# Attention head order and GpSimd's split: values of block 0 ahead of its scores, and a split that waits for the softmax

## The reference

```
hs = scan over 32 steps: GRU(h, x[:, t])                    # h0 = cond
q, k, v = hs @ Wq + bq, hs @ Wk + bk, hs @ Wv + bv          # 4 heads of 64
x = x + softmax(q k^T / 2) v @ Wo + bo                      # over the 32 steps
qs = scan over 32 steps: RK4(q, p, x[:, t], tanh(q) @ C^T)  # q0 = p0 = cond
x = x + bitlinear(silu(bitlinear(qs, Wg)) * bitlinear(qs, Wu), Wd)
```

## Time and profile before

| what | us |
|---|---|
| median of 3 runs | 613.3 |
| lowest and highest run | 613.23, 615.46 |
| profiled execution, its time | 614.01 |
| profiled execution, its span | 612.1 |
| TensorE busy | 578.9 (95%) |
| VectorE busy | 517.3 (85%) |
| ScalarE busy | 404.3 (66%) |
| GpSimd busy | 255.3 (42%) |

### The profile page before, as it was taken

How to read it: one execution, slowest core, us unless ns; L and a number is a source line. 1 busy time by engine, 2 the same in 40 slices (tenths; PEclk the granted TensorE clock), 3 DMA queues, 4 the chain that set the end, 5 groups by cost and what they waited for, 6 DMA issues and landing times.

```text
span 612.1 us, 14221 instructions
## 1 busy us (share of the span) xinstructions
PE 578.9 (95%) x4924; PEld 525.0 (86%) x4924; DVE 517.3 (85%) x1545; ACT 404.3 (66%) x982; POOL 255.3 (42%) x401
## 2 busy tenths in 40 slices
PE   9999999999999889988888999999999999999997
PEld 8999999999999878877776888887887887888885
DVE  3777677676777768898988999999999999999996
ACT  3554444545444456577446888988888888888785
POOL 0423233332322453420144455565565565565550
PEclk9999999999999999999999999999999999999999
DMA  8400000000000000500000000000000000000001
GB/s 264 175 3 1 1 2 2 1 1 2 1 1 1 19 1 1 187 1 1 2 0 2 10 11 18 19 16 12 19 19 11 19 18 9 18 20 11 18 19 35
DMA packets 12518, 14.88 MB, mean 24 GB/s; under 512 B 1632, under 2 KB 10144, under 8 KB 12448
## 3 DMA queue, kind: packets, MB, share of 16 engines
q1 hardware_dynamic: 12448, 13.97, 6.7%
HBM read 9.78 MB, written 4.19 MB: 23 GB/s over the span
## 4 chain that ended last, share of the span: by engine, by line
PE 71%; ACT 13%; DVE 12%; issue 3%; DMA 1%; POOL 0%; SPq 0%; DVEq 0%; ACTq 0%
PE PS L452 23%; PE PS L314 17%; PE PS L337 12%; ACT q_s L763 4%; PE PS L504 4%; PE PS L525 3%; ACT k_s L744 2%; PE PS L488 2%; PE PS L373 2%; ACT big L676 2%; PE PS L430 2%; PE PS L390 2%; DVE PS L1062 1%; DVE big L944 1%; ACT PS L747 1%
## 5 line engine op out<-in xcount | busy, mean ns | idle before, releaser
L452 PE MATMUL PS<-k_s,h_s 128*128 128x128 f32 x1024 | 160.8, 285 | 4.4 <-DVE PS L1042 1.9
L452 PEld LDWEIGHTS PS<-k_s,h_s 128*128 128x128 f32 x1024 | 131.7, 191 | 21.8 <-DVE PS L1050 9.8
L314 PE MATMUL PS<-part 128*128 128x256 f32 x900 | 115.6, 286 | 0.0
L314 PEld LDWEIGHTS PS<-part 128*128 128x128 f32 x900 | 109.8, 191 | 0.0
L744 ACT ACTIVATE k_s<-h_s 128x128 f32<-128x128 f32 x256 | 69.1, 306 | 50.6 <-DVE h_s L1147 29.1
L337 PE MATMUL PS<-big,wrk 128*128 128x128 f32 x744 | 88.4, 275 | 1.7 <-DVE big L901 1.7
L337 PEld LDWEIGHTS PS<-big,wrk 128*128 128x128 f32 x744 | 85.8, 192 | 2.3 <-DVE big L901 2.3
L1215 POOL COPY h_s<-big 128x256 f32<-128x256 f32 x32 | 21.4, 669 | 129.5 <-DVE big L901 129.5
L452 PE MATMUL PS<-h_s 128*128 128x128 f32 x384 | 74.2, 275 | 0.0
L452 PEld LDWEIGHTS PS<-h_s 128*128 128x128 f32 x384 | 58.3, 192 | 0.0
L641 ACT ACTIVATE big<-big 128x256 f32<-128x256 f32 x32 | 13.3, 416 | 63.2 <-DVE big L883 63.2
(11 more groups left out here) (188 smaller groups left out, 1273.1 us busy)
## 6 DMA issues: line engine op xcount, KB each, us to landing
out<-q_s SPq DMA_DIRECT2D x32, 128.0 KB, 1.7
x_s<-in_xT SPq DMA_DIRECT2D x14, 256.0 KB, 6.0
k_s<-in_wgT SPq DMA_DIRECT2D x1, 832.0 KB, 5.5
k_s<-in_wuT SPq DMA_DIRECT2D x1, 832.0 KB, 7.1
k_s<-in_wih SPq DMA_DIRECT2D x3, 256.0 KB, 4.5
wrk<-in_whh SPq DMA_DIRECT2D x3, 256.0 KB, 4.8
h_s<-in_wdT SPq DMA_DIRECT2D x1, 768.0 KB, 6.8
x_s<-in_xT SPq DMA_DIRECT2D x4, 128.0 KB, 4.0
```

The costliest lines, as they stand in the source:

```text
L314: r = pe.matmul(p, y, x, start=i == 0, stop=i == len(passes) - 1)
L452: return pe.matmul(PS[:, m, 0:128], w, x, start=False, stop=True, skip_group_check=True)
```

## The change

On TensorE, `values(0, 0)` is issued ahead of `scores(0)`. Its passes are reordered in all blocks, so that the four with the high part of the states come first and the two with the low part last; only in block 0 is there a wait for the low part between them. ScalarE copies the values of block 0 ahead of its scores. ScalarE now drains three of the four `last` banks (`last[0]`, `last[2]`, `last[3]`) and VectorE one (`last[1]`), after the low part of block 0's states. GpSimd's split `i`, for `i` from 1, additionally waits for `s_P >= i`, that is for the scaling of block `i - 1`, and its constants for `s_P >= 8`.

```diff
--- before.py
+++ after.py
@@ -365,8 +365,8 @@
                 if i:
                     pe.wait_ge(s_sc, i)
                 else:
-                    pe.wait_ge(s_qk, 62)
-                    pe.wait_ge(s_qka, 2)
+                    pe.wait_ge(s_qk, 61)
+                    pe.wait_ge(s_qka, 3)
                 for g in range(4):
                     for hd in range(4):
                         a, kk, at, u = 64 * (hd % 2), hd // 2, (4 * i + g) * 128, unit(g, hd)
@@ -378,15 +378,19 @@
                 hi, lo = v_hi[i % 2], v_lo[i % 2]
                 if (i, hf) == (0, 0):
                     pe.wait_ge(s_wv, 2)
-                    pe.wait_ge(s_vs0, 2)
+                    pe.wait_ge(s_vs0, 1)
+                    pe.wait_ge(s_qka, 1)
                 elif hf == 0:
                     pe.wait_ge(s_split, i)
                 if (i, hf) != (0, 0):
                     pe.wait_ge(s_V, 2 * i + hf)
                 for g in (2 * hf, 2 * hf + 1):
-                    passes = [(x[:, k, g * 128:(g + 1) * 128], w[:, k, :]) for k in range(2)
-                              for x, w in ((lo, wv_hi), (hi, wv_lo), (hi, wv_hi))]
+                    at = slice(g * 128, (g + 1) * 128)
+                    passes = [(hi[:, k, at], w[:, k, :]) for w in (wv_lo, wv_hi) for k in range(2)]
+                    passes += [(lo[:, k, at], wv_hi[:, k, :]) for k in range(2)]
                     for n, (x, w) in enumerate(passes):
+                        if (i, g, n) == (0, 0, 4):
+                            pe.wait_ge(s_vs0, 2)
                         r = pe.matmul(PS[:, 4, (g % 2) * 256:(g % 2) * 256 + 256], raw(x), raw(w), start=n == 0,
                                       stop=n == 5)
                 r.then_inc(s_Vp, 1)
@@ -431,8 +435,11 @@
                 r.then_inc(s_o, 1)
 
             for i in range(10):
+                if i == 0:
+                    values(0, 0)
                 if i < 8:
                     scores(i)
+                if 1 <= i < 8:
                     values(i, 0)
                 if i == 8:
                     feats_of(7)
@@ -654,12 +661,13 @@
             ac.activation(wsum[:, 3:4], ones[:, 0:1], ACT.Exp)
             ac.wait_ge(s_hb, T)
             ac.activation(raw(v_hi[0]), h_s[:, :, 0:512], ACT.Copy).then_inc(s_vs0, 1)
-            for u in last[2:]:
+            for u in (last[0], last[2], last[3]):
                 kind, j, i = u
-                dst = k_s[:, i % 2, :].rearrange("p (b t) -> p t b", t=T)[:, 2 * j:2 * j + 2, :]
+                w, m = divmod(i, 2)
+                dst = (q_s, k_s)[w][:, m, :].rearrange("p (b t) -> p t b", t=T)[:, 2 * j:2 * j + 2, :]
                 ac.wait_ge(s_bulk, number[u] + 1)
                 ac.activation(dst, bulk_bank(u).rearrange("p (t b) -> p t b", t=2), ACT.Identity,
-                              bias=ba[:, 1, i % 2:i % 2 + 1]).then_inc(s_qka, 1)
+                              bias=ba[:, w, m:m + 1]).then_inc(s_qka, 1)
 
             def keep_values(i, hf):
                 if i >= 2 and hf == 0:
@@ -704,8 +712,11 @@
                 if i == 8:
                     keep_feats(7)
                 if i < 8:
+                    if i == 0:
+                        keep_values(0, 0)
                     keep_scores(i)
-                    keep_values(i, 0)
+                    if i:
+                        keep_values(i, 0)
                     if i in (5, 6):
                         weight_round(i - 5)
                     if i:
@@ -913,10 +924,9 @@
                         ve.wait_ge(ld_x[(n + 2) // 2], 32)
                     at = (n + 2) * 256 + col
                     ve.tensor_copy(raw(x_hi[n % 2][:, :, col:col + B]), x_s[:, :, at:at + B]).then_inc(s_xhi, 1)
-            for u in last[:2]:
-                qk_out(u)
             ve.wait_ge(s_vs0, 1)
             ve.tensor_tensor(raw(v_lo[0]), h_s[:, :, 0:512], v_hi[0], ALU.subtract).then_inc(s_vs0, 1)
+            qk_out(last[1])
 
             def maximum(i):
                 ve.wait_ge(s_sc, i + 1)
@@ -1227,11 +1237,13 @@
             po_.wait_ge(s_hb, T)
             for r in range(2):
                 po_.memset(PT[r][:, :, :], 0.0).then_inc(s_zero, 1)
+
             for i in range(9):
                 if i < 7:
                     src, hi, lo = h_s[:, :, (i + 1) * 512:(i + 2) * 512], v_hi[(i + 1) % 2], v_lo[(i + 1) % 2]
                     if i:
                         po_.wait_ge(s_Vp, 2 * i)
+                        po_.wait_ge(s_P, i)
                     po_.tensor_copy(raw(hi), src).then_inc(s_vhi, 1)
                     if i == 0:
                         po_.wait_ge(s_bulk, number[last[-1]] + 1)
@@ -1240,6 +1252,7 @@
                 if i == 8:
                     po_.wait_ge(ld_coup, 16)
                     po_.wait_ge(s_Vp, 16)
+                    po_.wait_ge(s_P, 8)
                     po_.tensor_scalar(coupU, coup, U, 0.0, ALU.mult, ALU.add).then_inc(s_cp, 1)
                     for dst, f in ((id_q1, (1 - kap) / c4), (id_s2, -kap / c4), (id_z3, (2 - 2 * kap) / c4)):
                         po_.tensor_scalar(dst, ident[:, :], f, 0.0, ALU.mult, ALU.add).then_inc(s_cp, 1)
```

## The result

The changed kernel takes 611.94 us (median of 8 runs, 611.07 to 612.34), the kernel before 613.75 (8 runs, 613.23 to 615.48). The ratio is 0.9961 with a 95% interval of 0.9947 to 0.9975. That is 1.5 to 3.3 us faster, around 2.4. The ratio weighs every run and lies near that of the means (614.15 and 611.78); the medians alone differ by 1.8. The span of the profiled execution went from 612.1 to 609.5.

The account below looks back on a forecast made before the run. TensorE was taken to bound the middle of the attention stage, the only stage that can change. Terms +0.37 - 1.68 + 0 = -1.31 us, from a median of 613.3, gave 612.0 us; range 610.9 to 613.9.

Parts of the forecast that it names:

- The head: Start of the attention stage: scores 0 0.55 us later, 0.18 regained; +0.37 us in sum, carried through blocks 2 to 4.
- the 0.18 for the scaling: Block 0's softmax scaling on VectorE: 0.69 us instead of 0.87 once GpSimd's split waits, gaining 0.18.
- Block 4: Softmax scaling freed of GpSimd's subtraction, so L430 in block 5 comes earlier: 1.68 us gained.
- the 0.53 behind it: L430 in block 5 was to follow L410 by 0.53 us, as in the pair a block later.
- The end: Block 7: scaling loses 0.44 us of blocking, but VectorE then waits for ScalarE's copy; gain 0, bound 0 to 0.4.
- the wait of 0.1: A 0.1 us wait was to reappear at the L430 after block 5's, hidden by the chain through ScalarE and VectorE.
- The price of the wait: Delaying GpSimd's splits behind the scaling was to cost nothing, with 5 us of slack at block 2's reader.
- (a): Block 4's scaling stall, hanging on 10 ns, is absent from usual executions; only the head's cost remains: 613.7 us, chance 0.2.
- (b): L919, moved earlier at the head, is blocked by GpSimd's two memsets; scores 0 2.0 us late, 613.4 us, chance 0.1.
- (c): GpSimd's late work or ScalarE's new order costs another 0.3 to 0.8 us at the head: 612.5 us, chance 0.07.
- (d): VectorE does not bind the head and a 0.8 us lead survives, or 0.4 is kept at the end: 611.2 us, chance 0.08.

Follow-up runs that it names:

- waits only: Kernel before plus only GpSimd's added waits for the scaled softmax, head order unchanged; 611.85 us, ratio 0.9962 (again: 611.95 us, 0.9961).
- half ahead: Whole change, but six of values (0,0)'s twelve matmuls behind scores 0, and ScalarE copying scores 0 first; 611.87 us, ratio 0.9957.
- two waits: Kernel before plus two of GpSimd's added waits, for the splits beside the scaling of blocks 4 and 5; 612.42 us, ratio 0.9961.
- head only: Whole change without GpSimd's added waits; 618.16 us, ratio 1.0061.
- six idle matmuls: Kernel before plus six matmuls with unread results in TensorE's wait ahead of block 5's first weight sum; 613.74 us, ratio 0.9988.
- twelve idle matmuls: Kernel before plus twelve matmuls with unread results in TensorE's wait ahead of block 5's first weight sum; 614.89 us, ratio 1.0003.
- one wait: Kernel before plus one of GpSimd's added waits, for the split overlapping block 4's scaling; 613.79 us, ratio 0.9997.

## Why the prediction was right, and where it was short

The forecast of 612.0 met 611.94, and that it did so to 0.06 is partly luck. It stood on a base of 613.3, the median of three runs, where eight runs have 613.75; on that base the sum of -1.31 would have given 612.4. The base was 0.45 low and the gain 0.5 short (1.8 by the medians), and the two errors cancelled. The working was right in its signs. Two of its three terms had the wrong size, and one thing was not in it.

**The head.** Scores 0 were forecast 0.55 late and came 0.65 late: the drain of `last[0]` took 0.74, not 0.60, and TensorE waited 0.21 for it. The step from scores 0 to the maximum and the path through VectorE (projection (0,0) released by L960) were right, and so was the 0.18 for the scaling as far as projection (0,0): 0.65 - 0.18 = 0.47 against +0.48 measured there. What I had wrong is that this is carried through whole. The 0.18 is not: waits only is 0.15 early at projection (0,0), but 0.01 at projection (0,1) (+26.59, before +26.60), because VectorE then waits 0.42 instead of 0.29 for the copy of scores 2. The lateness is not, either. Projection (0,1) is only 0.37 late and the weighted sum of block 1 (before +28.19, after +28.46) 0.27, because before, projection (0,1) started (236.21) only as VectorE's residual ended (235.41 + 0.74 = 236.15); after, the residual ends at 234.92 + 0.75 = 235.67 and TensorE goes on by itself at 235.99. The projection itself took 1.66 before, behind this wait, and 1.55 after, which is the other 0.1. That this wait took up the difference is read from the rows and was not tried. From there +0.27 stays, so the term is +0.27 and not +0.37. Waits only against the change, +103.50 and +103.81, give 0.31 for the whole head. The rest of the argument is shown by half ahead.

**Block 4.** Forecast 1.68. From the weighted sum at +0.27 to projection (3,0) at -1.42 it is 1.69. That L410 (now L414) would be late next, and the 0.53 behind it, hold to 0.01.

**The end.** I took 0 with a bound of 0.4. The gain grows there from 1.42 to 1.59, by 0.17: VectorE's L960 still waits 0.26 for ScalarE, but the wait of 0.1 that I expected at block 6 did not come, and the scaling of block 7 is 0.44 shorter. The last gives the 0.17: in two waits, which leaves this scaling at 1.13, the gain is 1.68 at projection (3,0) and 1.66 at the integration. The sum becomes +0.27 - 1.69 - 0.17 = -1.59, where -1.31 was forecast.

**The clock.** The sum was one execution's. The page of the kernel before had full clock in every slice, and I read its 615.46 as spread. By its length that run was one with the lowered clock, the stall's second price: 1.8 us, in 31 of 64 executions. That is the part of the ratio that the sum lacks.

**The price of the wait.** "I price the delay at nothing" held for the place chosen. The reason that I gave, 5 us of slack at the reader, was not the reason that matters: 2.9 us later the reader still has slack, and it costs 2.1 us at projection (0,0) because GpSimd meets other instructions with two SBUF inputs.

**What I had not seen.** I treated the edits as independent. They are not, as head only shows: the new head lets GpSimd start 2.5 us sooner into block 0's maxima, and the wait prevents it. Head alone is 1.0061, waits alone 0.9962, together 0.9961. The gain is that of the waits; the head costs 0.3 us in the traces, which the times cannot tell.

**The rivals.** (a) falls: the stall was in both profiles of before and in that of six idle matmuls, all at 2.90. That it hangs on 10 ns is right all the same. In the kernel with twelve idle matmuls, the two started at 258.32 and 258.33, and there VectorE's took 0.69 and GpSimd's subtraction 2.93. How often this happens without a profile can be bounded: free of the stall, before would take about 611.9, and none of its 64 executions is below 612.65. (b) falls: L928 runs from 211.46 beside the memsets of 209.48 to 213.03 and takes 1.23. I had written that no such pair lies in the trace of before. One does: L919 started at 213.09, beside the memsets that end at 213.62, and took the same 1.22. The Trainium skill, "SBUF — State Buffer", section "Who interferes with whom", says that a VectorE instruction with two SBUF inputs does not contend with a GpSimd instruction that only writes SBUF; both rows agree. (c) and (d) did not come in the size given; the 611.2 of (d) is also no sum of its terms, since -0.8 - 1.7 gives 610.8, and the forecast with the 0.4 at the end 611.6.

## What to carry to other kernels

Where two engines can block each other, do not remove one collision alone: here one wait moved the stall a block on and gained nothing, and two waits brought nearly the whole gain. Before an engine is put ahead, ask which buffer it frees earlier and what then starts beside whom. When runs of one kernel fall in two groups, compare the granted clock of single executions: here a wait of 1.94 us on TensorE cost another 1.8 us in half of them. Six idle matmuls in it took that away without cost; twelve outlasted the wait and cost 1.0 us.

## What was not expected of the hardware

With the wait behind L935's stall it was 31 of 64; with six idle matmuls in it 0 of 12. Half ahead had it in 2 of 6, while its profile has none, so its place is open.
- A collision within 10 ns by the profile goes either way: 2.90 for VectorE with 258.06 and 258.07, 2.93 for GpSimd with 258.32 and 258.33. In each pair GpSimd's start is the earlier one; the second pair, from the kernel with twelve idle matmuls:

```profile
258.32 2.93 POOL L1241 TENSOR_TENSOR part<-h_s,part 128x1024 fp32r<-128x1024 f32 x1
258.33 0.69 DVE L937 TENSOR_TENSOR big<-big 128x512 f32<-128x512 f32 x1
```

- A stalled VectorE instruction ended 0.55 behind GpSimd's end, in all of the long stalls shown here (L935 at 258.07 and 267.94, L937 at 219.39, L1007 at 227.27), though alone it takes 0.69.
- The start of L353 differs between kernels with identical code ahead of it: 209.01 to 209.41 in six traces with the new head, 208.91 to 209.94 in eight without. This is larger than the 0.3 us that the head costs, and may be why the times of the change and of waits only do not differ; this was not tested. The cause was not looked for.
